# Adding the logarithm and relu terms of softplus on TensorE, by identity matmuls, instead of on VectorE

## Chip, cores and metric

The kernel runs on one core of a Trainium2 chip. The metric is the device time of one execution in microseconds (us), taken as the median of a few executions. A profile is one further execution, recorded by the hardware profiler.

## What is computed

The program is a network of two layers. Each layer has a state-space block (Mamba) over 2305 positions of 4 sequences, and then a mixture of experts. The change touches only the preparation of `dt` in the state-space block:

```python
dt = softplus(einsum('blr,dr->bld', dt, dt_proj_w) + dt_proj_b)     # the preparation
def step(h, (dt_t, B_t, C_t, u_t)):                                 # the scan over positions
    dA = exp(dt_t[:, :, None] * A)
    h = dA * h + (dt_t * u_t)[:, :, None] * B_t[:, None, :]
    y = einsum('bdn,bn->bd', h, C_t)
```

There are 128 inner channels and 16 states. softplus(v) is computed without overflow as relu(v) + ln(1 + e), with e = exp(-|v|). Because 1 + e is rounded, a correction rr = ((1 + e) - 1) - e is taken off the logarithm. So dt = ln(1 + e) - rr + relu(v).

## The kernel before

In each layer `phase_mamba` cuts every sequence into 5 chunks of 462 positions, so there are 20 chunks per layer and 40 in all. A chunk has 16 items (4 groups of channels by 4 groups of states, 128 rows each). The engines share an item like this, and each of them is a queue written out by hand, with semaphores between them:

- ScalarE writes the decay exp(dt*A) of the item into PSUM (line 647).
- GpSimd (POOL) forms the product dbu (line 700).
- VectorE scans decay and dbu over the positions (lines 782 and 785). For 10 items it multiplies the states by C itself, into `hc` (line 767). For the six items of `ON_POOL` GpSimd does it, into `hcp` (line 695).
- TensorE adds all 16 products into the PSUM bank `ysum` (line 558 for `hc`, 553 for `hcp`), in `SUM_ORDER`. The last three of that order are items 14 (`hc`), 13 (`hcp`) and 15 (`hc`).
- VectorE multiplies the finished `ysum` by the gate of the chunk (line 745), after the first scan of the next chunk.

While chunk k is scanned, chunk k+2 is prepared, spread over the queues by the `AT_` table. The preparation has a double PSUM buffer `front`: bank 0 takes the projections of u and dt, bank 1 those of z and of B and C. ScalarE writes `ab` = |v|, `rx` = relu(v) and `ex` = exp(-ab), then 1 + e into bank 0 (line 613), and after the decay of item 15 the logarithm into bank 1 (`prep_ln`, line 617). At the end of the chunk's program VectorE runs `prep_rr` (line 724) and `prep_dt` (line 731 takes `rr` off in PSUM, line 735 adds `rx` and writes `dd` in SBUF). GpSimd then multiplies `dd` by u (line 681), SyncE stores both to HBM and reads them back spread over the partitions as `rep`, and the next-but-one chunk scans with that. TensorE's next projection (`prep_u`, line 520) also waits for the end of `prep_dt`, since it overwrites `front`.

Two chunks are prepared before the loop (the prologue), in the same order of steps.

Of the kernel before, what the change touches and what calls it, by code (L numbers as in the profile page):

```python
# [14 lines left out]
ALU = mybir.AluOpType  # L15
ACT = mybir.ActivationFunctionType
AX_X = mybir.AxisListType.X

P = 128
# [13 lines left out]
TC = 462  # L33
# [21 lines left out]
HCD = 5  # L55


AT_SILU, AT_EXP, AT_ONE, AT_LN, AT_BC, AT_DT, AT_DTU, AT_Y = 6, 10, 11, 15, 13, 5, 3, 0
START = 16
NE, TOPK = 8, (2, 1)  # L60
F0, F1 = 512, 1024
# [14 lines left out]
def memory(nc, ctx, phase, used):  # L76

    def sb(name, shape, dt=F32):  # L80
        return ctx.enter_context(nc.sbuf_tensor(f"{phase}_{name}", shape, dt))

    def ps(name, shape, dt=F32):
        return ctx.enter_context(nc.psum_tensor(f"{phase}_{name}", shape, dt))

    def sem(name):
        used.append(nc.alloc_semaphore(f"{phase}_{name}"))
        return used[-1]

    return sb, ps, sem  # L90
# [297 lines left out]
def phase_mamba(nc, a, g, l):  # L388
# [4 lines left out]
    with ExitStack() as ctx:  # L393
        sb, ps, sem = memory(nc, ctx, f"mamba{l}", g["used"])
        T, m, sel = g["T"], g["mamba"][l], g["sel"]
        xs = sb("xs", [P, CW - 1])
        u, sz = sb("u", [P, UBUFS, TC]), sb("sz", [P, UBUFS, TC])
        ab, ex, rx, rr = sb("ab", [P, TC]), sb("ex", [P, TC]), sb("rx", [P, TC]), sb("rr", [P, TC])
        dd = sb("dd", [P, 2, TC])
        bc = sb("bc", [2 * DS, TC])  # L400

# [10 lines left out]
        ysum, front = ps("ysum", [P, BANK]), ps("front", [P, 2, BANK])  # L412

        xs_loaded, rep_loaded, bc_stored, dt_stored = sem("xs_loaded"), sem("rep_loaded"), sem("bc_stored"), sem("dt_stored")
        front_mm, front_act, front_dve, front_pool = sem("front_mm"), sem("front_act"), sem("front_dve"), sem("front_pool")
# [4 lines left out]
        y_ready, projected, added = sem("y_ready"), sem("projected"), sem("added")  # L420
        unshuffled, stats_ready, mv_ready = sem("unshuffled"), sem("stats_ready"), sem("mv_ready")
        half_ready, vare_ready, rstd_ready = sem("half_ready"), sem("vare_ready"), sem("rstd_ready")
        MM_U, MM_Z, MM_DT, MM_BC, MMS = 1, 2, 3, 4, 4
        A_U, A_Z, A_ABS, A_RELU, A_EXP, A_ONE, A_BC, A_LN, ACTS = 1, 2, 3, 4, 5, 6, 7, 8, 8
        D_R, D_LR, D_DT, DVES = 1, 2, 3, 3
        REPS = 2 * NS
        block = ctx.enter_context(nc.Block())

        def chunk_of(eng, tile, k):

            if isinstance(k, int):
                return tile[:, k % UBUFS, :]
            return tile[:, bass.ds(eng.snap(k % UBUFS), 1), :]
# [78 lines left out]
        @block.tensor  # L512
        def _(pe):
            for s in (front_mm, hc_summed, hcp_summed, projected):
                pe.sem_inc(s, START)

            def prep_u(k):
                pe.wait_ge(xs_loaded, 32 * (k + 1))
                pe.wait_ge(front_dve, START + DVES * k)
                nc.tensor.matmul(front[:, 0, 0:TC], m["wu"][:, 0, :], xs[:, 0:TC], start=True, stop=False)  # L520
                nc.tensor.matmul(front[:, 0, 0:TC], m["wu"][:, 1, :], xs[:, 2:2 + TC],
                                 start=False, stop=True).then_inc(front_mm, 1)

            def prep_z(k):
                nc.tensor.matmul(front[:, 1, 0:TC], m["wz"][:, :], xs[:, 2:2 + TC],
                                 start=True, stop=True).then_inc(front_mm, 1)

            def prep_dt(k):
                pe.wait_ge(front_act, START + ACTS * k + A_Z)
                nc.tensor.matmul(front[:, 0, 0:TC], m["wdt"][:, :], chunk_of(pe, u, k),  # L530
                                 start=True, stop=True).then_inc(front_mm, 1)

            def prep_bc(k):
                nc.tensor.matmul(front[0:2 * DS, 1, 0:TC], m["wbc"][:, :], chunk_of(pe, u, k),
                                 start=True, stop=True).then_inc(front_mm, 1)

            for k in range(2):
                prep_u(k)
                prep_z(k)
                prep_dt(k)  # L540
                prep_bc(k)
            with pe.Fori(0, NCH) as k:
                prep_u(k + 2)
                prep_z(k + 2)

                pe.wait_ge(y_ready, START + k)
                nc.tensor.matmul(ysum[:, 0:TC], m["diag"][:, :], chunk_of(pe, u, k), start=True, stop=False)
                for at, i in enumerate(SUM_ORDER):
                    end = at == ITEMS - 1
                    if i in ON_POOL:  # L550
                        n = ON_POOL.index(i)
                        pe.wait_ge(hcp_ready, START + NP_ * k + n + 1)
                        nc.tensor.matmul(ysum[:, 0:TC], sel[:, i // NM, :], hcp[:, n % HCP, :],  # L553
                                         start=False, stop=end).then_inc(hcp_summed, 1)
                    else:
                        n = ON_DVE.index(i)
                        pe.wait_ge(hc_ready, START + ND * k + n + 1)
                        nc.tensor.matmul(ysum[:, 0:TC], sel[:, i // NM, :], hc[:, n % HCD, :],  # L558
                                         start=False, stop=end).then_inc(hc_summed, 1)
                    if at == AT_DT:  # L560
                        prep_dt(k + 2)
                    if at == AT_DT + 1:
                        prep_bc(k + 2)

            pe.wait_ge(front_dve, START + DVES * (NCH + 2))
            for t in range(NT):
                b, j = divmod(t, TPB)
                pe.wait_ge(unshuffled, R * (b + 1))
                pe.wait_ge(added, START + t - 1)
                out = front[0:TT, t % 2, 0:C].rearrange("p (c q) -> p q c", q=R * R)  # L570
                for q in range(R * R):
                    mm = nc.tensor.matmul(out[:, q, :], yp[:, b % 2, q, j * TT:(j + 1) * TT], m["wout"][:, :],
                                          start=True, stop=True, skip_group_check=True)
                mm.then_inc(projected, 1)
# [8 lines left out]
        def _(act):  # L583
            act.sem_inc(front_act, START)
            act.sem_inc(decay_ready, START)
            at = act.alloc_register(f"act_row{l}")
# [26 lines left out]
                nc.scalar.activation(front[:, 0, 0:TC], ex[:, :], ACT.Copy, bias=1.0).then_inc(front_act, 1)  # L613

            def prep_ln(k):
                act.wait_ge(front_act, START + ACTS * k + A_BC)
                nc.scalar.activation(front[:, 1, 0:TC], ex[:, :], ACT.Ln, bias=1.0).then_inc(front_act, 1)

            def prep_bc(k):
                act.wait_ge(front_mm, START + MMS * k + MM_BC)  # L620
# [4 lines left out]
            for k in range(2):  # L625
                prep_silu(k)
                prep_exp(k)
                prep_one(k)
                prep_bc(k)
                prep_ln(k)  # L630
            nc.scalar.preload_act_table_set("exp_and_others")
            with act.Fori(0, NCH // 2) as pair:
                for par in range(2):
                    k = pair * 2 + par
# [82 lines left out]
        def _(dve):  # L717
# [8 lines left out]

            def prep_dt(k):
                done = START + DVES * k
                dve.wait_ge(front_act, START + ACTS * k + A_LN)
                dve.wait_ge(front_dve, done + D_R)  # L730
                nc.vector.tensor_tensor(front[:, 1, 0:TC], front[:, 1, 0:TC], rr[:, :], ALU.subtract).then_inc(front_dve, 1)
                if not (isinstance(k, int) and k == 0):
                    dve.wait_ge(dt_stored, 16 * NG * k)
                dve.wait_ge(front_dve, done + D_LR)
                nc.vector.tensor_tensor(dd[:, 0, :], front[:, 1, 0:TC], rx[:, :], ALU.add).then_inc(front_dve, 1)

            for k in range(2):
                prep_rr(k)
                prep_dt(k)
# [10 lines left out]
            with dve.Fori(0, B) as b:  # L750
# [4 lines left out]
                with dve.Fori(0, CPB) as c:  # L755
                    k = dve.snap(b * CPB + c)
# [17 lines left out]
                    for i in range(ITEMS):  # L774
                        done = START + ITEMS * k + i
# [15 lines left out]
                    read_out(ITEMS - 1)  # L791
                    prep_rr(k + 2)
                    prep_dt(k + 2)

            gate(NCH)
# [645 lines left out]
def build(nc, a):  # L1441
    with ExitStack() as ctx:
# [16 lines left out]
        for l in range(2):  # L1459
            phase_sequence(nc, a, g, l)  # L1460
            phase_mamba(nc, a, g, l)
            with ExitStack() as ffn:
                weights, phase_experts = ((weights0, phase_experts0), (weights1, phase_experts1))[l]
                g["xn"] = ffn.enter_context(nc.sbuf_tensor(f"xn{l}", [TT, NT, C], F32))
                w, prefetch = weights(nc, a, g, ffn)
                phase_route(nc, a, g, l, prefetch)
                phase_experts(nc, a, g, w)
            if l == 0:

                nc.clear_and_free_semaphores(g["used"])  # L1470
                g["used"].clear()
                nc.all_engine_barrier()  # L1472
# [40 lines left out]
```

## Time and profile before

| | |
|---|---|
| median of 3 executions | 2142.44 us (2141.5 to 2144.28) |
| the profiled execution's own time | 2142.27 us |
| its span in the profile | 2140.6 us |
| VectorE (DVE) busy | 1279.3 us, 60% |
| TensorE (PE) busy | 1574.8 us, 74% |
| GpSimd (POOL) busy | 1159.7 us, 54% |
| ScalarE (ACT) busy | 1027.7 us, 48% |

These are averages over a state-space loop and an experts stage in each layer, which have different limits. The page's 40 slices show VectorE at nine tenths or more through both state-space loops and at one or two tenths in much of the experts stages. "Idle before, releaser" in a row is how long the engine had nothing to do before the instruction, and what let it go on. A float32 matmul of the program is two records in the trace ("x2").

### The profile page before, as it was taken

How to read it: one execution, taken by the hardware profiler on the slowest of the kernel's cores; microseconds unless marked ns; L12 is line 12 of the kernel's file. 1: busy time of each engine (PE TensorE's matmuls, PEld its weight loads, DVE VectorE, ACT ScalarE, POOL GpSimd, SP SyncE). 2: the span in 40 equal slices, each digit the busy share in tenths (PEclk: the TensorE clock that was granted, in tenths of full speed). 3: DMA queues.
4: the chain of work that ended last, by engine and by line, in shares of the span. 5: the costliest groups of instructions: out<-in, count | busy, mean ns of one | idle time of the engine just before them, and what ended most of it. 6: DMA issues, size and time to landing. Idle time of an engine off the chain costs nothing. (4 is left out here: it accounts for less than half of the span.)

```text
span 2140.6 us, 26276 instructions
## 1 busy us (share of the span) xinstructions
PE 1574.8 (74%) x4872; PEld 813.1 (38%) x4873; DVE 1279.3 (60%) x2268; ACT 1027.7 (48%) x1696; POOL 1159.7 (54%) x1151
## 2 busy tenths in 40 slices
PE   4477777777786389999971367777777778199993
PEld 3122222222255146666640122222222228166661
DVE  4399999999976001111117279999999996111102
ACT  5577777777751022232321367777777762021111
POOL 2399999999941700000017179999999991400004
PEclk9799999999975699999995689999999995599995
DMA  6687777777735342111113487777777772123323
GB/s 215 145 177 175 174 176 175 174 174 173 170 85 194 92 137 69 44 44 47 47 47 99 122 181 175 173 177 176 173 174 174 171 170 88 55 71 112 111 65 97
DMA packets 104909, 283.48 MB, mean 132 GB/s; under 512 B 19788, under 2 KB 78428, under 8 KB 94012
## 3 DMA queue, kind: packets, MB, share of 16 engines
q1 hardware_dynamic: 96680, 265.34, 51.2%
q0 software_dynamic: 8192, 17.71, 2.8%
q8 instruction: 15, 0.25, 0.0%
q14 instruction: 22, 0.18, 0.0%
HBM read 225.80 MB, written 57.18 MB: 132 GB/s over the span
## 5 line engine op out<-in xcount | busy, mean ns | idle before, releaser
L700 POOL TENSOR_TENSOR mamba_dbu<-mamba_rep 128x462 f32<-128x462 f32 x640 | 676.4, 1084 | 69.7 <-DMA mamba_rep<-dt_rows 66.0
L558 PE MATMUL mamba_ysum<-mamba_hc,all_sel 128*128 128x462 f32 x800 | 420.6, 608 | 239.3 <-DVE mamba_hc L767 238.5
L647 ACT ACTIVATE mamba_state<-mamba_rep,all_m_acol 128x462 f32<-128x462 f32 x640 | 388.8, 638 | 228.1 <-DVE mamba_last L782 227.2
L785 DVE TENSOR_TENSOR_SCAN mamba_state<-mamba_state,mamba_carry,mamba_dbu 128x462 f32<-128x462 f32 x400 | 455.2, 1176 | 7.3 <-ACT mamba_state L647 7.3
L558 PEld LDWEIGHTS mamba_ysum<-mamba_hc,all_sel 128*128 128x128 f32 x800 | 125.9, 192 | 520.0 <-DVE mamba_hc L767 503.3
L782 DVE TENSOR_TENSOR_SCAN mamba_last<-mamba_state,mamba_last,mamba_dbu 128x462 f32<-128x462 f32 x240 | 280.7, 1170 | 30.2 <-ACT mamba_state L647 17.0
L695 POOL TENSOR_TENSOR mamba_hcp<-mamba_last,mamba_rep 128x462 f32<-128x462 f32 x240 | 266.6, 1111 | 35.0 <-DVE mamba_last L782 28.3
L1237 DVE TENSOR_TENSOR experts_h<-experts_sg,experts_up 128x512 f32<-128x512 f32 x62 | 42.6, 688 | 370.2 <-PE experts_up L1132 312.3
L767 DVE TENSOR_TENSOR mamba_hc<-mamba_state,mamba_rep 128x462 f32<-128x462 f32 x400 | 249.6, 627 | 0.0
L553 PE MATMUL mamba_ysum<-mamba_hcp,all_sel 128*128 128x462 f32 x480 | 238.3, 579 | 0.0
L290 POOL MEMSET seq_mhalf<- 96x3 f32 x2 | 0.2, 98 | 360.8 <-POOLq L1472 360.8
L1152 PE MATMUL experts_down<-weights_wd,experts_hT 128*128 x496 | 119.2, 384 | 40.1 <-issue 39.3
L553 PEld LDWEIGHTS mamba_ysum<-mamba_hcp,all_sel 128*128 128x128 f32 x480 | 90.9, 196 | 113.4 <-issue 110.5
L1152 PEld LDWEIGHTS experts_down<-weights_wd,experts_hT 128*128 128x128 f32 x496 | 95.1, 192 | 79.9 <-issue 69.9
L1384 POOL DMA_DIRECT2D expert_rows<-experts_eo x8 | 6.6, 826 | 217.2 <-DVE experts_eo L1374 217.2
L647 ACT ACT_TABLE_LOAD x80 | 102.6, 1283 | 38.2 <-DMA mamba_rep<-dt_rows 37.4
L1132 PE MATMUL experts_gate<-weights_wgu,experts_xT 128*128 x248 | 118.3, 600 | 3.5 <-ACT experts_xT L1188 2.9
L1207 ACT ACTIVATE experts_eo<-experts_down 128x256 f32<-128x256 f32 x62 | 23.8, 383 | 196.0 <-PE experts_down L1152 168.7
L1014 POOL DMA_INDIRECT slot_rows<-xn,all_slot x72 | 66.5, 923 | 94.0 <-issue 60.2
L1132 PE MATMUL experts_up<-weights_wgu,experts_xT 128*128 x248 | 116.7, 593 | 0.0
L1350 ACT ACTIVATE experts_hT<-experts_hid,weights_b 128x432 f32<-128x432 f32 x64 | 39.6, 620 | 156.0 <-PE experts_hid L1324 156.0
L1333 PE MATMUL experts_down<-weights_w,experts_hT 128*108 128x256 f32 x512 | 112.5, 380 | 1.2 <-ACT experts_hT L1350 0.7
(175 smaller groups left out, 2165.9 us busy)
## 6 DMA issues: line engine op xcount, KB each, us to landing
mamba_rep<-bc_rows SPq DMA_DIRECT2D x168, 462.0 KB, 7.0
mamba_rep<-dt_rows SPq DMA_DIRECT2D x168, 462.0 KB, 7.4
dt_rows<-mamba_dd SPq DMA_DIRECT2D x168, 115.5 KB, 7.6
weights_w<-in_L_w_dram SPq DMA_DIRECT2D x16, 1024.0 KB, 9.0
mamba_xs<-seq_scratch SPq DMA_DIRECT2D x92, 116.0 KB, 9.3
experts_xs<-slot_rows SPq DMA_DIRECT2D x62, 128.0 KB
expert_rows<-experts_eo SPq DMA_DIRECT2D x62, 128.0 KB, 1.7
slot_rows<-setup_zero SPq DMA_DIRECT2D x11, 512.0 KB
```

Of the source, the lines that this page charges most:

```text
L553: nc.tensor.matmul(ysum[:, 0:TC], sel[:, i // NM, :], hcp[:, n % HCP, :], start=False, stop=end).then_inc(hcp_summed, 1)
L558: nc.tensor.matmul(ysum[:, 0:TC], sel[:, i // NM, :], hc[:, n % HCD, :], start=False, stop=end).then_inc(hc_summed, 1)
L647: nc.scalar.activation(state[:, STATE_BANK[i], 0:TC], rep[:, par * REP_ROWS + i // NM, :], ACT.Exp, scale=m["acol"][:, i:i + 1]).then_inc( ...
L695: pool.tensor_tensor(hcp[:, n % HCP, :], last[:, n, :], rep[:, first + 3 * NG + i % NM, :], ALU.mult).then_inc(hcp_ready, 1)
L700: pool.tensor_tensor(dbu[:, i % 4, :], rep[:, first + NG + i // NM, :], rep[:, first + 2 * NG + i % NM, :], ALU.mult).then_inc(dbu_ready, 1)
L767: nc.vector.tensor_tensor(hc[:, n % HCD, :], state[:, STATE_BANK[i], 0:TC], rep[:, bass.ds(c_rows + 3 * NG + i % NM, 1), :], ALU.mult).the ...
L782: nc.vector.tensor_tensor_scan(last[:, n, :], bank, dbu[:, i % 4, :], last[:, n, TC - 1:TC], ALU.mult, ALU.add).then_inc(scan_done, 1)
L785: nc.vector.tensor_tensor_scan(bank, bank, dbu[:, i % 4, :], carry[:, i:i + 1], ALU.mult, ALU.add).then_inc(scan_done, 1)
L1014: pool.indirect_dma_start(out=g["xs"][:, :], out_offset=bass.IndirectOffsetOnAxis(ap=g["slot"][:, c, t:t + 1], axis=0), in_=g["xn"][:, t, ...
L1132: mm = nc.tensor.matmul(bank[:, par, :], xT[:, par, k * P:(k + 1) * P], wgu[:, bass.ds(e, 1), which, k, :], start=(k == 0), stop=(k == 1))
L1152: mm = nc.tensor.matmul(down[:, par, 0:C], hT[:, par, f * P:(f + 1) * P], wd[:, bass.ds(e, 1), f, :], start=(f == 0), stop=(f == FC0 - 1))
L1333: mm = nc.tensor.matmul(down[0:CT, i % 2, 0:C], hT[:, f, i * CT:(i + 1) * CT], w2[:, par, f, :], start=(f == 0), stop=(f == FC1 - 1))
```

## The change

TensorE gets a step `prep_add`: two matmuls with the identity as weights that put `ln` and `rx` into bank 1 of `front` and add them there. VectorE's pass of line 731 goes away, and its last pass takes `rr` off that sum. ScalarE writes the logarithm into a new SBUF tile `ln` instead of PSUM, and its wait in front of it goes away. `prep_add` stands on TensorE after the matmul at place 14 of `SUM_ORDER` (`AT_ADD`), which is item 13, and before that of item 15; it waits for the logarithm.

```diff
-AT_SILU, AT_EXP, AT_ONE, AT_LN, AT_BC, AT_DT, AT_DTU, AT_Y = 6, 10, 11, 15, 13, 5, 3, 0
+AT_SILU, AT_EXP, AT_ONE, AT_LN, AT_BC, AT_DT, AT_DTU, AT_Y, AT_ADD = 6, 10, 11, 15, 13, 5, 3, 0, 14
...
+            def prep_add(k):
+                pe.wait_ge(front_act, START + ACTS * k + A_LN)
+                nc.tensor.matmul(front[:, 1, 0:TC], g["ident"][:, :], ln[:, :], start=True, stop=False)
+                nc.tensor.matmul(front[:, 1, 0:TC], g["ident"][:, :], rx[:, :], start=False, stop=True).then_inc(front_mm, 1)
...
                 prep_bc(k)
+                prep_add(k)
...
                     if at == AT_DT + 1:
                         prep_bc(k + 2)
+                    if at == AT_ADD:
+                        prep_add(k + 2)
...
             def prep_ln(k):
-                act.wait_ge(front_act, START + ACTS * k + A_BC)
-                nc.scalar.activation(front[:, 1, 0:TC], ex[:, :], ACT.Ln, bias=1.0).then_inc(front_act, 1)
+                nc.scalar.activation(ln[:, :], ex[:, :], ACT.Ln, bias=1.0).then_inc(front_act, 1)
...
             def prep_dt(k):
                 done = START + DVES * k
-                dve.wait_ge(front_act, START + ACTS * k + A_LN)
-                dve.wait_ge(front_dve, done + D_R)
-                nc.vector.tensor_tensor(front[:, 1, 0:TC], front[:, 1, 0:TC], rr[:, :], ALU.subtract).then_inc(front_dve, 1)
+                dve.wait_ge(front_mm, START + MMS * k + MM_ADD)
                 if not (isinstance(k, int) and k == 0):
                     dve.wait_ge(dt_stored, 16 * NG * k)
-                dve.wait_ge(front_dve, done + D_LR)
-                nc.vector.tensor_tensor(dd[:, 0, :], front[:, 1, 0:TC], rx[:, :], ALU.add).then_inc(front_dve, 1)
+                dve.wait_ge(front_dve, done + D_R)
+                nc.vector.tensor_tensor(dd[:, 0, :], front[:, 1, 0:TC], rr[:, :], ALU.subtract).then_inc(front_dve, 1)
```

TensorE's queue at the end of the loop over chunks, before. The first row is item 14, then items 13 and 15.

```order
L558 MATMUL mamba_ysum<-mamba_hc,all_sel 128x462 [waits mamba0_hc_ready]
L552 REGISTER_ALU
L553 MATMUL mamba_ysum<-mamba_hcp,all_sel 128x462 [waits mamba0_hcp_ready]
L557 REGISTER_ALU
L558 MATMUL mamba_ysum<-mamba_hc,all_sel 128x462 [waits mamba0_hc_ready]
```

The same place in the changed kernel:

```order
L565 MATMUL mamba_ysum<-mamba_hc,all_sel 128x462 [waits mamba0_hc_ready]
L559 REGISTER_ALU
L560 MATMUL mamba_ysum<-mamba_hcp,all_sel 128x462 [waits mamba0_hcp_ready]
L539 REGISTER_ALU
L540 MATMUL mamba_front<-mamba_ln,all_ident 128x462 [waits mamba0_front_act]
L541 MATMUL mamba_front<-mamba_rx,all_ident 128x462
L564 REGISTER_ALU
L565 MATMUL mamba_ysum<-mamba_hc,all_sel 128x462 [waits mamba0_hc_ready]
```

The two adds stand behind the matmuls of items 14 and 13, and item 15 now stands behind the adds.

VectorE's queue at the end of the loop, before, from the product of item 15 on:

```order
L767 TENSOR_TENSOR mamba_hc<-mamba_state,mamba_rep 128x462 [waits mamba0_hc_summed]
L723 ISA
L724 SCALAR_TENSOR_TENSOR mamba_rr<-mamba_front,mamba_ex 128x462 [waits mamba0_front_act]
L729 REGISTER_ALU
L730 ISA [waits mamba0_front_act]
L731 TENSOR_TENSOR mamba_front<-mamba_front,mamba_rr 128x462 [waits mamba0_front_dve]
L733 REGISTER_ALU
L734 REGISTER_ALU [waits mamba0_dt_stored]
L735 TENSOR_TENSOR mamba_dd<-mamba_front,mamba_rx 128x462 [waits mamba0_front_dve]
L755 REGISTER_ALU
```

And in the changed kernel:

```order
L773 TENSOR_TENSOR mamba_hc<-mamba_state,mamba_rep 128x462 [waits mamba0_hc_summed]
L731 ISA
L732 SCALAR_TENSOR_TENSOR mamba_rr<-mamba_front,mamba_ex 128x462 [waits mamba0_front_act]
L737 ISA
L739 REGISTER_ALU [waits mamba0_front_mm]
L740 ISA [waits mamba0_dt_stored]
L741 TENSOR_TENSOR mamba_dd<-mamba_front,mamba_rr 128x462 [waits mamba0_front_dve]
L761 REGISTER_ALU
```

One pass is gone, and the one that is left waits for TensorE (`front_mm`); the loop's next scan stands behind it.

## Rows read from the trace of the kernel before

**Rows 1.** Windows: busy time per engine in the loops of both layers.

```profile
core 0: us, PE busy (x) PEld busy (x) DVE busy (x) ACT busy (x) POOL busy (x), PEclk, DMA share, GB/s
...
94.00:618.00 524.00, 403.28 (x879) 146.63 (x877) 511.73 (x727) 374.05 (x558) 484.95 (x459) 0.98 0.78 174
...
1245.00:1770.00 525.00, 404.09 (x878) 147.11 (x877) 511.68 (x727) 374.98 (x559) 484.16 (x459) 0.98 0.78 173
```

**Rows 2.** Groups by line: VectorE's two passes of `prep_dt`.

```profile
L731 DVE TENSOR_TENSOR mamba_front<-mamba_front,mamba_rr 128x462 f32<-128x462 f32 x44 | 28.5, 647 | 8.2 <-ACT mamba_front L617 6.8
...
L735 DVE TENSOR_TENSOR mamba_dd<-mamba_front,mamba_rx 128x462 f32<-128x462 f32 x44 | 28.1, 640 | 1.6
```

**Rows 3.** Timeline of VectorE over one chunk's end: start, us, instruction, [idle before].

```profile
277.27 1.18 DVE L782 TENSOR_TENSOR_SCAN mamba_last<-mamba_state,mamba_last,mamba_dbu 128x462 f32<-128x462 f32 x1 [0.32 <-issue]
...
300.54 0.64 DVE L767 TENSOR_TENSOR mamba_hc<-mamba_state,mamba_rep 128x462 f32<-128x462 f32 x1
301.09 0.64 DVE L724 SCALAR_TENSOR_TENSOR mamba_rr<-mamba_front,mamba_ex 128x462 f32<-128x462 f32 x1
301.76 0.65 DVE L731 TENSOR_TENSOR mamba_front<-mamba_front,mamba_rr 128x462 f32<-128x462 f32 x1
302.44 0.64 DVE L735 TENSOR_TENSOR mamba_dd<-mamba_front,mamba_rx 128x462 f32<-128x462 f32 x1
303.40 1.18 DVE L782 TENSOR_TENSOR_SCAN mamba_last<-mamba_state,mamba_last,mamba_dbu 128x462 f32<-128x462 f32 x1 [0.32 <-issue]
304.49 0.61 DVE L745 TENSOR_TENSOR mamba_y<-mamba_ysum,mamba_sz 128x462 f32 x1
```

**Rows 4.** Timeline of TensorE over the same end.

```profile
300.63 1.04 PE L558 MATMUL mamba_ysum<-mamba_hc,all_sel 128*128 128x462 f32 x2 [0.88 <-DVE mamba_hc L767]
301.51 0.94 PE L553 MATMUL mamba_ysum<-mamba_hcp,all_sel 128*128 128x462 f32 x2
302.28 0.94 PE L558 MATMUL mamba_ysum<-mamba_hc,all_sel 128*128 128x462 f32 x2
303.14 1.04 PE L520 MATMUL mamba_front<-mamba_xs,all_m_wu 128*128 128x462 f32 x2
```

**Rows 5.** Timeline of ScalarE there: the logarithm, then the next chunk's decays.

```profile
298.16 0.56 ACT L617 ACTIVATE mamba_front<-mamba_ex 128x462 f32<-128x462 f32 x1
...
300.47 1.78 ACT L647 ACTIVATE mamba_state<-mamba_rep,all_m_acol 128x462 f32<-128x462 f32 x3
```

**Rows 6.** Timeline of GpSimd there.

```profile
299.24 4.21 POOL L700 TENSOR_TENSOR mamba_dbu<-mamba_rep 128x462 f32<-128x462 f32 x4 [0.64 <-DMA mamba_rep<-dt_rows]
303.68 1.00 POOL L681 TENSOR_TENSOR mamba_dd<-mamba_dd,mamba_u 128x462 f32<-128x462 f32 x1 [0.23 <-issue]
```

**Rows 7.** Timeline: end of the first layer's loop, VectorE released by TensorE.

```profile
616.70 0.94 PE L558 MATMUL mamba_ysum<-mamba_hc,all_sel 128*128 128x462 f32 x2
...
617.67 0.64 DVE L745 TENSOR_TENSOR mamba_y<-mamba_ysum,mamba_sz 128x462 f32<-128x462 f32 x1 [0.17 <-PE mamba_ysum L558]
```

**Rows 8.** Timeline: the prologue of the first layer.

```profile
67.55 0.56 ACT L617 ACTIVATE mamba_front<-mamba_ex 128x462 f32<-128x462 f32 x1
...
68.82 0.64 DVE L735 TENSOR_TENSOR mamba_dd<-mamba_front,mamba_rx 128x462 f32<-128x462 f32 x1
...
69.60 1.88 PE L520 MATMUL mamba_front<-mamba_xs,all_m_wu 128*128 128x462 f32 x2 [6.65 <-DVE mamba_dd L735]
...
71.28 1.75 PE L521 MATMUL mamba_front<-mamba_xs,all_m_wu 128*128 128x462 f32 x2
...
83.73 0.65 DVE L731 TENSOR_TENSOR mamba_front<-mamba_front,mamba_rr 128x462 f32<-128x462 f32 x1 [1.70 <-ACT mamba_front L617]
...
84.48 0.64 DVE L735 TENSOR_TENSOR mamba_dd<-mamba_front,mamba_rx 128x462 f32<-128x462 f32 x1
```

**Rows 9.** Windows and timeline of TensorE: a low-clock stretch (columns: busy, clock, DMA share, GB/s).

```profile
284.61:285.61 1.00, 1.00 (x3) 0.50 0.47 91
...
284.54 1.75 PE L553 MATMUL mamba_ysum<-mamba_hcp,all_sel 128*128 128x462 f32 x2
```

More of the change, by code:

```diff
@@ L398, in phase_mamba @@
         ab, ex, rx, rr = sb("ab", [P, TC]), sb("ex", [P, TC]), sb("rx", [P, TC]), sb("rr", [P, TC])
+        ln = sb("ln", [P, TC])
         dd = sb("dd", [P, 2, TC])
@@ L422, in phase_mamba @@
         half_ready, vare_ready, rstd_ready = sem("half_ready"), sem("vare_ready"), sem("rstd_ready")
-        MM_U, MM_Z, MM_DT, MM_BC, MMS = 1, 2, 3, 4, 4
+        MM_U, MM_Z, MM_DT, MM_BC, MM_ADD, MMS = 1, 2, 3, 4, 5, 5
         A_U, A_Z, A_ABS, A_RELU, A_EXP, A_ONE, A_BC, A_LN, ACTS = 1, 2, 3, 4, 5, 6, 7, 8, 8
-        D_R, D_LR, D_DT, DVES = 1, 2, 3, 3
+        D_R, D_DT, DVES = 1, 2, 2
         REPS = 2 * NS
```

## The prediction

> **What bounds the kernel now.** I first read the page's slices: VectorE is full only in the two state-space loops, and the change touches nothing else. The windows of these loops [rows 1] give the limit there: VectorE is busy 511.73 of 524 us and 511.68 of 525 us, next to 485 us of GpSimd, 403 us of TensorE and 374 us of ScalarE. So an added or removed microsecond on VectorE, busy or waiting, is a microsecond of the kernel, as long as no other engine takes over. The timeline of VectorE over one chunk [rows 3] shows the period: the first scan of one chunk starts at 277.27 us and that of the next at 303.40 us, so 26.13 us a chunk. The reader should look at its last four instructions: the product of item 15 (300.54), `rr` (301.09 to 301.73), the pass of line 731 (301.76) and that of line 735 (302.44 to 303.08). The next scan starts at 303.40, which is 0.96 us after line 735 started. There is hardly an idle gap. Then I read the other queues at the same moment, since the new pass waits for one of them: TensorE [rows 4], ScalarE [rows 5], GpSimd [rows 6].
>
> **The change, part by part.**
>
> *VectorE loses line 731.* It lasts 0.647 us [rows 2] and its successor starts 0.68 us after it (301.76 to 302.44, [rows 3]). Taken alone this gives 40 x 0.68 = 27 us back. The pass that is left reads PSUM and SBUF and writes SBUF, as line 735 does now, so it takes 0.64 us [rows 2].
>
> *ScalarE.* The logarithm goes to SBUF instead of PSUM, 0.56 us [rows 5]. It ends at 298.72 and nothing asks for it before 301.7, so the other destination and the dropped wait cost nothing. The cover is 3 us; the decays that follow have their own cover, since those of the next chunk start at 300.47 for a scan at 303.40.
>
> *TensorE gets two matmuls, and where they stand decides the case.* Their inputs are there early, but the queue is in order: they stand behind the matmul of item 14, which waits for VectorE's product of that item and starts at 300.63 [rows 4], and behind that of item 13 (301.51). Item 15 starts at 302.28, and there the first add will start. Price of an add: it is a float32 matmul of 128x128 weights by 462 columns, the shape of lines 553 and 558, and one that follows another starts 302.28 - 301.51 = 0.77 us after it; the last one's end is 0.94 us after its start [rows 4]. So the `ln` add starts at 302.28, the `rx` add at 303.05 and ends at 303.99. That the weights are the identity changes nothing in it that a row shows, so the 0.77 us of the row goes into the sum. The Trainium skill (TensorE: Matmul & The Clock Gate, Back-to-back issue gap) gives N/2.4 + 2.5 ns for a matmul at full clock, which for N = 462 is an estimated 0.195 us; by that the adds would end about 1.2 us earlier and the loop's part of the sum would be some 20 us. The trace does not agree for float32: its 0.77 us is four times as much. The skill's FP8 and Floating Point Precision (TensorE Precision Notes) gives true FP32 four passes, and with those the trace agrees.
>
> *The new wait on VectorE.* How soon VectorE goes on after TensorE is in the rows at the loop's end [rows 7]: the last matmul ends at 616.70 + 0.94 = 617.64 and the gate starts at 617.67, 0.03 us later. In the changed queue a wait and a further wait instruction stand between the semaphore and the pass. The nearest row is in the prologue [rows 8]: line 731 ends at 84.38 and line 735, with such an instruction ahead of it, starts at 84.48, 0.10 us later, against 0.03 us in the loop. I take 0.10, with 0 and 0.2 as bounds. So the pass starts at 303.99 + 0.10 = 304.09. Line 735 starts at 302.44 now. Everything behind it (the 0.96 us to the next scan, the loop's branch and registers) moves with it, so the chunk gets 304.09 - 302.44 = **1.65 us longer** (1.55 to 1.75), the missing pass already counted: VectorE ends `rr` at 301.73 and then waits 2.36 us for something that replaces 0.68 us. This recurs in every one of the 40 chunks: 40 x 1.65 = **66.0 us** (62 to 70).
>
> *What queues behind, and who is late next.* Behind the waiting pass on VectorE are all scans of the next chunk. TensorE's item 15 moves to 303.83 to 304.77; its reader is the gate, now at 304.49 [rows 3], which moves with the scans to 306.14, so 1.3 us are left. TensorE's next projection (303.14, [rows 4]) waits for the pass, so it moves by the same 1.65 us, to 304.79, and item 15 is just done. GpSimd's product of `dd` starts at 303.68 now [rows 6] and cannot start before about 304.8, so +1.1 us, and its stores and the `rep` transfer behind it move by as much. The transfer lands 0.64 us after GpSimd asks for it (299.24), and the decays it feeds begin at 300.47 [rows 5], for a scan at 303.40. The first is over at about 301.1 (1.78/3 = 0.6), so 2.3 us are spare; it arrives 1.1 later, and the scan that needs it comes 1.65 later, so the margin grows. No second stall follows. All other work in a chunk hangs on VectorE's scans and moves with them.
>
> *The prologue.* For chunk 0 the chain is logarithm, `prep_dt`, GpSimd, store, replicate, first scan, and VectorE waits at its end anyway. The logarithm ends at 68.11 and line 735 starts at 68.82 [rows 8]. Afterwards the adds start at about 68.18. TensorE will have been idle for over 5 us, and after 6.65 us of idleness the row at 69.60 is at the low clock: 1.68 us to the next pair's start, and that pair 1.75 us. At those rates the adds end at 68.18 + 3.43 = 71.61 and the pass starts at 71.71, so +2.9 us; at the full clock of [rows 4] (0.88 + 0.94) it is +1.3. I take the low clock, 2 layers x 2.9 = **5.8 us** (2.6 to 5.8). Chunk 1's preparation moves too, but ends before the replicated rows of chunk 0 arrive.
>
> *The sum.* 66.0 + 5.8 = 71.8 us. Against the profiled execution's own time, 2142.27 us, this is 2214.1 us; the median of the runs shown is 0.2 us above that, so 2214.2, and I say 2214.
>
> **The rivals.**
>
> 1. *Forecast, slower by about 72 us.* Chance 0.84. Its own range is 62 + 2.6 to 70 + 5.8, so 2207 to 2218; a few chunks with a low clock at their end (rival 2's price of 3.1 us, three times) make the upper end 2227.
>
> 2. *TensorE's clock falls at the end of the chunk.* Now a chunk in the loop has a low stretch in some places early in it: clock 0.50, which is 1.2 GHz, and a pair of 1.75 us in place of 0.94 [rows 9], behind a stretch in which TensorE mostly waited for VectorE's products. It costs nothing there, because no one waits for these sums. If that met the four matmuls that the pass now waits for, they would take 1.68 + 1.54 + 1.54 + 1.75 = 6.5 us in place of 3.36, +3.1 us each time. The windows have the mean clock at 0.98 in the loops [rows 1], so about 4% of 1049 us, 42 us, is at the low level. A low microsecond on these matmuls delays VectorE by half a microsecond, so if all of it fell there the kernel would lose 21 us more, 2235 us; in every chunk it would be 124 us. Against it: the chunk's end is TensorE's densest part, and the period changes only by 6%. Chance 0.06.
>
> 3. *The other side: the adds are hidden.* If they ended before `rr` does (301.73), the missing pass would be pure gain: 2142.4 - 27 = 2115 us, less 1 for the prologue. For that they would have to end 2.3 us earlier than I find; a saving starts where they end before about 302.3 (the pass would start before 302.44). That needs them ahead of item 14's wait in the queue, since even item 14's and item 13's matmuls take until 302.28. The order of the changed program has them behind. It stays possible only if the modelled ends and starts of the matmuls mislead by over 1.6 us. Chance 0.04.
>
> 4. *An add is cheaper than the row*: one record and not two, half the price, 0.39 us each. The pass then starts 0.77 us earlier, 0.88 us per chunk, 35 us and some 4 us in the prologue, 2181 us. All matmuls of this shape are two records [rows 4], so 0.04. (The skill's formula above would make an add cheaper still, and the estimate some 2165 us.)
>
> 5. *It cancels out.* VectorE's delay would have to be taken from a wait elsewhere in the loop; its idle time in the whole loop is 12 us of 524 [rows 1]. 2142 us, chance 0.02.
>
> **How the numbers follow.** The likeliest case gives 2214. The range 2205 to 2227 holds it with its bounds and a few low-clock ends, and leaves out rivals 2 to 5 (0.16). A change within 0.2% (4 us) is what a measurement of this kernel can hardly tell from none. Slower: rivals 1, 2 and 4, 0.94. Within 0.2%: 0.02. Faster: 0.04.
>
> **What the profile of the changed kernel would show.** The period between first scans near 27.8 us; the last VectorE pass of a chunk with about 2.3 us idle before it, released by TensorE; that wait about 94 us over 40 chunks; the adds starting 1.65 us after item 14's start with 0.77 us between them; GpSimd's product of `dd` waiting for VectorE; VectorE's busy time down by 44 x 0.647 = 28.5 us, while the span grows. I would be wrong if the adds showed a start before 302.28 relative to item 14, or if a wait for the `rep` transfer appeared on VectorE's first scan.

## The result, and the profile after

The changed kernel takes 2215.07 us (median of 4 runs, 2212.71 to 2216.69), the kernel before 2141.97 us (median of 4, 2138.43 to 2144.28). The ratio is 1.0342, with a 95% interval of 1.0324 to 1.036: the change makes the kernel 73 us slower. The prediction said 2214 us, slower.

The first thing to look at is the end of a chunk on VectorE in the changed kernel. This timeline answers to [rows 3]; its columns are start, us, instruction, [idle before].

```profile
289.94 1.18 DVE L788 TENSOR_TENSOR_SCAN mamba_last<-mamba_state,mamba_last,mamba_dbu 128x462 f32<-128x462 f32 x1 [0.33 <-issue]
...
313.21 0.64 DVE L773 TENSOR_TENSOR mamba_hc<-mamba_state,mamba_rep 128x462 f32<-128x462 f32 x1
313.76 0.64 DVE L732 SCALAR_TENSOR_TENSOR mamba_rr<-mamba_front,mamba_ex 128x462 f32<-128x462 f32 x1
316.90 0.64 DVE L741 TENSOR_TENSOR mamba_dd<-mamba_front,mamba_rr 128x462 f32<-128x462 f32 x1 [2.50 <-PE mamba_front L541]
317.87 1.18 DVE L788 TENSOR_TENSOR_SCAN mamba_last<-mamba_state,mamba_last,mamba_dbu 128x462 f32<-128x462 f32 x1 [0.33 <-issue]
318.96 0.61 DVE L751 TENSOR_TENSOR mamba_y<-mamba_ysum,mamba_sz 128x462 f32 x1
```

Where `rr` was followed at once by two passes, it is followed by 2.50 us of nothing and one pass. From the product of item 15 to the last pass it is now 316.90 - 313.21 = 3.69 us; it was 1.90. The period, from first scan to first scan, is 317.87 - 289.94 = 27.93 us in place of 26.13, so 1.80 us more. It is the same in all chunks but those in which a new sequence starts (0.4 us longer, before and after alike) or the loop has just begun (up to 0.2 us longer).

TensorE at the same place answers to [rows 4]:

```profile
313.30 1.04 PE L565 MATMUL mamba_ysum<-mamba_hc,all_sel 128*128 128x462 f32 x2 [0.88 <-DVE mamba_hc L773]
314.18 0.94 PE L560 MATMUL mamba_ysum<-mamba_hcp,all_sel 128*128 128x462 f32 x2
314.95 0.94 PE L540 MATMUL mamba_front<-mamba_ln,all_ident 128*128 128x462 f32 x2
315.73 0.94 PE L541 MATMUL mamba_front<-mamba_rx,all_ident 128*128 128x462 f32 x2
316.50 0.94 PE L565 MATMUL mamba_ysum<-mamba_hc,all_sel 128*128 128x462 f32 x2
317.59 1.04 PE L521 MATMUL mamba_front<-mamba_xs,all_m_wu 128*128 128x462 f32 x2 [0.15 <-DVE mamba_dd L741]
```

The adds stand where the order of the queue put them: items 14 and 13 first, then the two adds at distances of 0.77 us, and item 15 behind. The inputs of the adds had been ready since the logarithm's end, at 310.83 + 0.59 = 311.42 in the timeline of ScalarE:

```profile
310.83 0.59 ACT L625 ACTIVATE mamba_ln<-mamba_ex 128x462 f32<-128x462 f32 x1
```

The groups by line, with the idle time ahead of them and its releaser, give the sum over all chunks:

```profile
L689 POOL TENSOR_TENSOR mamba_dd<-mamba_dd,mamba_u 128x462 f32<-128x462 f32 x42 | 45.7, 1088 | 157.5 <-DVE mamba_dd L741 157.5
...
L540 PE MATMUL mamba_front<-mamba_ln,all_ident 128*128 128x462 f32 x88 | 45.2, 597 | 20.9 <-ACT mamba_ln L625 20.9
L541 PE MATMUL mamba_front<-mamba_rx,all_ident 128*128 128x462 f32 x88 | 44.5, 590 | 0.0
L741 DVE TENSOR_TENSOR mamba_dd<-mamba_front,mamba_rr 128x462 f32<-128x462 f32 x44 | 28.2, 640 | 120.9 <-PE mamba_front L541 120.9
```

VectorE waited 120.9 us for the second add: four times 5.23 us in the prologues, and 100 us in the 40 chunks. TensorE waited for the logarithm only in the prologues, 4 times 5.2 us. VectorE's busy time fell from 1279.3 to 1251.1 us, as it had to, and the kernel got slower.

Where the 74.4 us between the two profiled spans (2215.0 and 2140.6 us) are, by the timelines of VectorE: from the first scan to the last gate of a loop it was 523.99 and 523.77 us and is 559.66 and 559.53 us, so 71.4 us are in the two loops. The two stretches from the first `rr` to the first scan are 0.2 and 0.8 us shorter (27.88 to 27.66 us, and 28.39 to 27.59), which is about as much as traces with the same prologue differ: e5 below, whose prologue is that of the kernel before, has 27.23 and 27.66 us. The remaining 4.0 us are spread over stages that the change does not touch; the four executions after lie 4 us apart themselves.

### The profile page after: what moved, and what is told of

The parts are those of the page before. It is cut to its first block and busy times, and to the rows that moved or that the text cites. A ratio compares the mean times of both kernels' runs of the same rounds, so it can differ in the third digit from the quotient of the medians.

```text
span 2215.0 us, 26542 instructions
## 1 busy us (share of the span) xinstructions
PE 1656.1 (75%) x5048; PEld 852.1 (38%) x5049; DVE 1251.1 (56%) x2224; ACT 1029.1 (46%) x1696; POOL 1159.6 (52%) x1151
## 5 line engine op out<-in xcount | busy, mean ns | idle before, releaser
L689 POOL TENSOR_TENSOR mamba_dd<-mamba_dd,mamba_u 128x462 f32<-128x462 f32 x42 | 45.7, 1088 | 157.5 <-DVE mamba_dd L741 157.5
L1356 ACT ACTIVATE experts_hT<-experts_hid,weights_b 128x432 f32<-128x432 f32 x64 | 39.7, 620 | 156.5 <-PE experts_hid L1330 156.5
```

## The experiments

Ten kernels were run. Each is compared with the kernel before on the same chip, because the chips differ: the kernel before took 2093.68 and 2095.46 us on two of them and 2139.81 us on a third. The time saved on the faster chips is in the stretches outside the two loops: e7 below, run on one of them, has the changed kernel's period of 27.93 us, and its loops take 559.59 and 559.50 us, where the changed kernel's took 559.66 and 559.53. So the table gives the difference of the medians on one chip, and the period between first scans that most chunks of the trace have. e7 is not in it, since it was executed once only.

| kernel | median, us | before, same chip | difference | ratio (95%) | period |
|---|---|---|---|---|---|
| changed kernel | 2215.07 | 2141.97 | +73.1 | 1.0342 (1.0324 to 1.036) | 27.93 |
| e3 adds behind item 15 | 2195.83 | 2093.68 | +102.2 | 1.0491 (1.0472 to 1.0509) | 28.70 |
| e2 adds ahead of item 13 | 2136.58 | 2093.68 | +42.9 | 1.0205 (1.0188 to 1.0222) | 27.15 |
| e1 adds ahead of item 14 | 2076.4 | 2093.68 | -17.3 | 0.9912 (0.9898 to 0.9927) | 25.67 |
| e4 TensorE's wait last | 2156.78 | 2093.68 | +63.1 | 1.0303 (1.0284 to 1.0322) | 27.72 |
| e5 wait, no adds | 2167.77 | 2139.81 | +28.0 | 1.0122 (1.0106 to 1.0139) | 26.84 |
| e6 one add | 2179.49 | 2139.81 | +39.7 | 1.0187 (1.017 to 1.0204) | 27.15 |
| e9 pass removed, nothing added | 2118.18 | 2139.81 | -21.6 | 0.9898 (0.9881 to 0.9914) | 25.56 |
| e10 e1, wait last, gate later | 2119.03 | 2139.81 | -20.8 | 0.9904 (0.9887 to 0.992) | 25.57 |
| e11 e1, gate later | 2069.13 | 2095.46 | -26.3 | 0.9875 (0.9858 to 0.9891) | 25.46 |

The main theory (A) was that the place of the adds in TensorE's queue is the cost. Its rival (B) was that handing work to TensorE, or its added work, costs wherever it stands.

**e1, e2, e3: the place alone.** One number of the table that sets the order is changed.

```diff
-..., AT_Y, AT_ADD = 6, 10, 11, 15, 13, 5, 3, 0, 14
+..., AT_Y, AT_ADD = 6, 10, 11, 15, 13, 5, 3, 0, 12      # e1; 13 in e2, 15 in e3
```

e1, ahead of item 14:

> Theory A (the place in TensorE's queue): the adds now stand ahead of item 14's matmul, so they start when item 11's is done, 299.58 us in the terms of the trace of before, and end at 301.29, before rr ends at 301.73. VectorE's last pass follows rr with no wait, the chunk loses the missing pass, 0.68 us: period 25.45 us, and 40 x 0.68 = 27 us less than the kernel before, 2115 us. Theory B (TensorE's part costs as such: the handover to it, or its added 1.7 us of work per chunk): the pass still waits about as in the changed kernel, period 27.9, 2215 us. Theory C (the place matters, but something else becomes the bound once VectorE is shorter: GpSimd, busy 24 us of a period, or the replicated rows): between 2120 and 2142 us with a new wait on VectorE's scans.

e2, between items 14 and 13:

> The adds stand between item 14's matmul and item 13's, one matmul earlier than in the changed kernel. Theory A: VectorE's pass starts 0.77 us earlier in each chunk, period 27.93 - 0.77 = 27.16 us, 40 x 0.77 = 31 us less than the changed kernel, 2184 us. Theory B: no difference, 2215 us.

e3, behind item 15:

> The adds stand behind item 15's matmul, one matmul later than in the changed kernel. Theory A: period 27.93 + 0.77 = 28.70 us, 31 us more than the changed kernel, 2246 us. Theory B: no difference, 2215 us.

Measured: the periods of e2 and e3 are 27.15 and 28.70 us, 0.78 less and 0.77 more than the changed kernel, one matmul each way. e1 is faster than the kernel before. So the same two matmuls, the same handover and the same VectorE work give +102, +73, +43 or -17 us by their place alone, and B falls. But e1 has 25.67 us in most chunks and 25.45 only in a few, 17 us gained and not 27: C is partly true, though neither of its candidates is. The wait is not on a scan: the first scan still starts 0.96 us behind the last pass, as before, and the 0.32 us of idle time in its row, which the profile puts down to ScalarE here, was there before too [rows 3]. VectorE's and TensorE's timelines in e1 show where the rest went. The adds end at 271.19 + 0.94 = 272.13, before `rr` does (272.56), and the pass follows `rr` at once, as expected:

```profile
271.93 0.63 DVE L732 SCALAR_TENSOR_TENSOR mamba_rr<-mamba_front,mamba_ex 128x462 f32<-128x462 f32 x1
272.59 0.64 DVE L741 TENSOR_TENSOR mamba_dd<-mamba_front,mamba_rr 128x462 f32<-128x462 f32 x1
273.55 1.18 DVE L788 TENSOR_TENSOR_SCAN mamba_last<-mamba_state,mamba_last,mamba_dbu 128x462 f32<-128x462 f32 x1 [0.32 <-ACT mamba_state L655]
274.85 0.64 DVE L751 TENSOR_TENSOR mamba_y<-mamba_ysum,mamba_sz 128x462 f32 x1
...
271.19 0.94 PE L541 MATMUL mamba_front<-mamba_rx,all_ident 128*128 128x462 f32 x2
...
273.52 0.94 PE L565 MATMUL mamba_ysum<-mamba_hc,all_sel 128*128 128x462 f32 x2
```

The gate (line 751) starts 1.30 us after the first scan; before it was 1.09 [rows 3]. It needs the sum with item 15, whose matmul ends at 273.52 + 0.94 = 274.46, just before the gate would have been due (274.64), with three instructions of VectorE's queue between that wait and the gate. Nothing marks it as idle in the row; the reader finds it by comparing starts. That this delay is what is missing is tested by e10 and e11.

**e4: the order of VectorE's waits.** In the changed kernel the pass starts 316.90 - (315.73 + 0.94) = 0.23 us after the second add's modelled end, where I had taken 0.10.

```diff
-                dve.wait_ge(front_mm, START + MMS * k + MM_ADD)
                 if not (isinstance(k, int) and k == 0):
                     dve.wait_ge(dt_stored, 16 * NG * k)
                 dve.wait_ge(front_dve, done + D_R)
+                dve.wait_ge(front_mm, START + MMS * k + MM_ADD)
```

> The changed kernel with the three waits of VectorE's last pass in another order: the wait for TensorE is the last and sits on the pass itself, so no wait instruction stands between the semaphore and the pass. In the changed kernel the pass starts 0.23 us after the second add's modelled end. If the two instructions in between are part of that, it starts 0.03 to 0.1 us after it, period 27.73 to 27.80, 5 to 8 us less than the changed kernel, 2207 to 2210 us. If the 0.23 us is the handover itself, the period stays 27.93 and the time 2215 us.

```profile
287.21 0.64 DVE L741 TENSOR_TENSOR mamba_dd<-mamba_front,mamba_rr 128x462 f32<-128x462 f32 x1 [2.30 <-PE mamba_front L541]
...
286.23 0.94 PE L541 MATMUL mamba_front<-mamba_rx,all_ident 128*128 128x462 f32 x2
```

Now it is 287.21 - 287.17 = 0.04 us, the period is 27.72 us, 0.21 less, and the difference to the kernel before is 63 us in place of 73. Two instructions of the queue are gone from between TensorE's semaphore and the pass, the one that carried this wait (line 739) and the one with the wait for the stores (line 740); together they cost 0.2 us, so 0.1 us each. The handover itself costs next to nothing. The 10 us are more than the 5 to 8 expected; the two differences come from different chips, and 40 times the 0.21 us is 8.

The order in the code is not always that of the queue. In the prologues, where the waits are for constants and not for registers, it is the other way round: the pass starts 0.04 us after the second add in the changed kernel and 0.11 to 0.14 us after it in e4, whose trace has a wait instruction between them there.

**e5: the wait without the adds.** The kernel before, with one more wait in front of line 731.

```diff
                 dve.wait_ge(front_dve, done + D_R)
+                if not isinstance(k, int):
+                    dve.wait_ge(hcp_summed, START + NP_ * (k - 1))
                 nc.vector.tensor_tensor(front[:, 1, 0:TC], front[:, 1, 0:TC], rr[:, :], ALU.subtract).then_inc(front_dve, 1)
```

> The kernel before, both VectorE passes kept, no adds on TensorE; only the first pass (line 731) also waits until TensorE has summed item 13. Theory A (order of TensorE's queue): that matmul ends at 302.45 us in the trace of before, and with no instruction between the wait and the pass VectorE starts 0.03 us later, 302.48, where it starts at 301.76: 0.72 us per chunk, period 26.85, 29 us more than the kernel before. With the 0.23 us seen in the changed kernel it would be 0.9 us and 37 us. Theory B (the adds themselves, through TensorE's load, clock or PSUM): no adds, so no difference to the kernel before.

Measured: period 26.84 us, 0.71 us more than before, +28 us. Theory A's figure was 0.72 and 29 us. The first pass (here line 733) starts 0.03 us after item 13's matmul ends (278.70 + 0.94 = 279.64):

```profile
278.29 0.63 DVE L724 SCALAR_TENSOR_TENSOR mamba_rr<-mamba_front,mamba_ex 128x462 f32<-128x462 f32 x1
279.67 0.65 DVE L733 TENSOR_TENSOR mamba_front<-mamba_front,mamba_rr 128x462 f32<-128x462 f32 x1 [0.75 <-PE mamba_ysum L553]
...
278.70 0.94 PE L553 MATMUL mamba_ysum<-mamba_hcp,all_sel 128*128 128x462 f32 x2
```

Without any work added to TensorE, being behind item 13 alone costs VectorE this much.

**e6: one add.** The changed kernel without the second matmul (the relu term is left out of dt).

> The changed kernel with one identity matmul instead of two: the relu term is left out of dt. If an add costs a whole float32 matmul of 0.77 us on the way to VectorE, the period falls from 27.93 to 27.16 us and the time is 43 us above the kernel before, in place of 73. If the handover and the wait for item 13 are the cost and the adds are nearly free, it stays within 5 us of the changed kernel.

Measured: period 27.15 us, 0.78 less than in the changed kernel, +39.7 us (43 expected; 40 times the 1.02 us over the period before is 41). The price of an add on this path is a whole float32 matmul. So the changed kernel's loop adds up from measured parts: e5's wait behind item 13 (0.71), two adds (2 x 0.78), two instructions behind the wait (0.21), less the missing pass (0.68), 1.80 us, which is what the periods say.

**e9: the pass removed and nothing in its place.** The kernel before without line 731 (the correction `rr` is left out of dt; it is still computed).

> The kernel before without VectorE's pass of line 731 and with nothing in its place (the correction rr is left out of dt). This is the most that taking one pass off VectorE can bring: theory A expects 0.68 us per chunk, period 25.45, 27 us below the kernel before. If another engine or the replicated rows bound the shorter chunk, the period is above 25.45 and VectorE's first scan waits for them.

Measured: 25.56 us and -21.6 us, not 25.45 and -27. Neither an engine nor the replicated rows are late, since the first scan starts 0.97 us behind the last pass, as ever. The last pass starts 0.75 us after `rr`, in place of 0.66 in e1:

```profile
271.04 0.62 DVE L724 SCALAR_TENSOR_TENSOR mamba_rr<-mamba_front,mamba_ex 128x462 f32<-128x462 f32 x1
271.79 0.64 DVE L733 TENSOR_TENSOR mamba_dd<-mamba_front,mamba_rx 128x462 f32<-128x462 f32 x1
272.76 1.18 DVE L780 TENSOR_TENSOR_SCAN mamba_last<-mamba_state,mamba_last,mamba_dbu 128x462 f32<-128x462 f32 x1 [0.33 <-ACT mamba_state L647]
```

In my edit the wait for the stores stood behind the wait for `rr`. It is the 0.1 us of e4 again, now behind another wait; no run of this kernel with the waits exchanged was made, but e10 and e11 differ in that way alone.

**e10 and e11: the gate one scan later.** Both have e1's place and `AT_Y` = 1; e10 also has e4's order of waits, e11 that of the changed kernel.

```diff
-..., AT_Y, AT_ADD = 6, 10, 11, 15, 13, 5, 3, 0, 14
+..., AT_Y, AT_ADD = 6, 10, 11, 15, 13, 5, 3, 1, 12
```

> The changed kernel with the adds ahead of item 14, the wait for TensorE last, and the gate one scan later in VectorE's queue. With the adds ahead of item 14 the period was mostly 25.67 us and not 25.45, and the gate started 1.30 us after the chunk's first scan in place of 1.09, since TensorE ended item 15 only just before. If that late sum is all that was missing, the gate behind the second scan finds it done, the period is 25.45 in nearly all chunks, and the time is 26 to 28 us below the kernel before, against 17 us with the gate where it was. If GpSimd or the replicated rows hold the chunk, it stays at 25.67 and 17 us.

Measured for e10: 25.57 us in nearly every chunk, -20.8 us, between the two outcomes that were expected. The gate's delay is gone, but the last pass starts 0.77 us after `rr`: with the adds early, `rr` and not TensorE comes last, and e4's order puts an instruction behind that wait. So e11:

> The changed kernel with the adds ahead of item 14 and the gate one scan later, and VectorE's three waits in the order of the changed kernel, so that the wait for rr sits on the pass itself. With the wait for TensorE last the pass started 0.76 us after rr, with this order and the adds ahead 0.66 us. If each instruction between the wait that ends last and the pass costs 0.1 us, the period falls from 25.57 to about 25.46 us and the time is 24 to 26 us below the kernel before, against 21 us. If the other rows' order does not matter, it stays at 25.57 and 21 us.

```profile
270.85 0.62 DVE L732 SCALAR_TENSOR_TENSOR mamba_rr<-mamba_front,mamba_ex 128x462 f32<-128x462 f32 x1
271.51 0.64 DVE L741 TENSOR_TENSOR mamba_dd<-mamba_front,mamba_rr 128x462 f32<-128x462 f32 x1
272.46 1.18 DVE L788 TENSOR_TENSOR_SCAN mamba_last<-mamba_state,mamba_last,mamba_dbu 128x462 f32<-128x462 f32 x1 [0.31 <-ACT mamba_state L655]
273.56 1.16 DVE L791 TENSOR_TENSOR_SCAN mamba_state<-mamba_state,mamba_carry,mamba_dbu 128x462 f32<-128x462 f32 x1
274.63 0.62 DVE L751 TENSOR_TENSOR mamba_y<-mamba_ysum,mamba_sz 128x462 f32 x1
```

Measured: 25.46 us, -26.3 us, ratio 0.9875. The last pass follows `rr` by 0.66 us and the gate is not late. This is the gain that taking one pass off VectorE can bring (0.68 us x 40 = 27 us), and e11 beats both kernels.

**e7: a longer prologue.** In the changed kernel the prologue got no longer, against my 5.8 us. The queue of SyncE shows why; its rows are the issues of transfers. Before:

```profile
67.91 1.73 SPq L468 DMA_DIRECT2D mamba_rep<-bc_rows  x4
70.72 2.59 SPq L461 DMA_DIRECT2D dt_rows<-mamba_dd  x4
80.33 1.72 SPq L476 DMA_DIRECT2D mamba_rep<-dt_rows  x4
```

After:

```profile
68.22 1.73 SPq L469 DMA_DIRECT2D mamba_rep<-bc_rows  x4
73.89 2.60 SPq L462 DMA_DIRECT2D dt_rows<-mamba_dd  x4
80.51 1.72 SPq L477 DMA_DIRECT2D mamba_rep<-dt_rows  x4
```

Counted from the first `rr` (65.80 us before, 66.12 after), the stores of dt are issued 2.9 us later (7.77 us in place of 4.92), but the replication that waits for them is issued 0.1 us earlier (14.39 in place of 14.53). In e7 TensorE does two extra `ln` matmuls in front of the adds, in the prologue alone; nothing else changes.

```diff
                 prep_bc(k)
+                pe.wait_ge(front_act, START + ACTS * k + A_LN)
+                for _ in range(2):
+                    nc.tensor.matmul(front[:, 1, 0:TC], g["ident"][:, :], ln[:, :], start=True, stop=True)
                 prep_add(k)
```

> The changed kernel with two more identity matmuls ahead of the adds of the two chunks of the prologue, nothing else; about 3.1 us more on that chain at the low clock. In the changed kernel the chain got 3.2 us longer at the stores of dt, but the first scan still came 27.7 us after the first rr, as before (27.9). Theory D (the dt rows' stores wait behind the transfer that replicates B and C, so the first 3 us are hidden, and only what goes beyond shows): the first scan comes 29 to 31 us after the first rr. Theory E (nothing of this chain is on the path to the first scan): it stays at 27.4 to 28.2 us. The loop's period is 27.93 us in either.

```profile
68.39 1.73 SPq L469 DMA_DIRECT2D mamba_rep<-bc_rows  x4
76.61 2.60 SPq L462 DMA_DIRECT2D dt_rows<-mamba_dd  x4
80.94 1.72 SPq L477 DMA_DIRECT2D mamba_rep<-dt_rows  x4
```

e7 was executed once (2168.97 us), so only its trace is used. Its stores are issued 10.32 us after the first `rr` (66.29 us), 5.4 us later than before and 2.5 us later than in the changed kernel, and the replication of dt at 14.65 us after it. From the first issue of these stores to that of the replication the three kernels took 9.6, 6.6 and 4.3 us in the first layer and 9.9, 6.3 and 5.6 us in the second. From the issue of the B and C replication to that of dt they took 12.4, 12.3 and 12.6 us in the first layer, and 12.7, 12.0 and 13.5 us in the second. So all of the changed kernel's 2.9 us was hidden in front of the replication in both layers. Of e7's further delay of the stores 0.3 of 2.5 us reached the replication in the first layer, and 1.5 of 2.2 us in the second. In the first layer the stores themselves took a median of 8.0, 5.1 and 2.6 us from issue to landing, and from 70 to 76 us the profile has the DMA engines fully busy in all three traces, at 219 to 232 GB/s. That fits theory D, that the stores wait behind that transfer; whether by their order in the queue or because the engines are busy is open, since neither the queues nor the transfer were changed.

The first scan comes 28.5 and 29.3 us after the first `rr` in the two layers. The first is short of D's range of 29 to 31, and both are above E's 28.2. In the changed kernel it was 27.7 and 27.6 us, and the other traces lie between 27.2 and 28.0 us in the first layer and between 27.5 and 28.4 in the second. The period stayed at 27.93 us.

## Why the prediction was right, step by step

**What bounds the kernel.** Right: in every variant of the table the time moved by about 40 times what VectorE's period moved by, within 2.1 us.

**The place of the adds and their price.** Right. The wait for item 14's product, item 13's matmul and 0.77 us per add appear as worked out, and e2, e3 and e6 measure single matmuls on this path (0.78, 0.77 and 0.78 us) and e5 the wait behind item 13 without the adds (0.71 us). The quick formula of the Trainium skill (TensorE: Matmul & The Clock Gate, Back-to-back issue gap), by which an add would have been an estimated 0.2 us, does not give the float32 matmuls here, which measure 0.77 to 0.78.

**The new wait's latency.** This term was mis-sized: 0.10 us taken, 0.23 measured, and above the bound of 0.2. The row that I used had one instruction behind the wait, the changed loop has two, line 739 with the wait itself and line 740 (e4). With it the period grew by 1.80 and not 1.65 us, and the loops by 71.4 and not 66.0 us; 1.80 also lies just above my 1.55 to 1.75.

**The prologue.** Wrong in its effect: the chain up to the stores did get 2.9 us longer, as worked out, at the low clock (the adds took 68.51 to 71.95, 3.44 us against my 3.43), but the step "VectorE waits at its end anyway", taken to mean that the delay reaches the first scan, failed. The replication behind the stores was issued no later; the stores seem to wait for another transfer, which fits e7 but is not proven. 5.8 us predicted, none found (0.2 and 0.8 us less).

These two errors have opposite signs. The loops came out 5.4 us over, the prologues 6.8 us under, and the stages outside, for which I had said nothing, gave 4.0 us more in the profiled pair. That the total of 2214 is within 1 us of the median is in part luck; the direction and the size of the loop's term are not.

**What queues behind.** Right: item 15 and the gate moved with the scans (the gate 1.09 us after the first scan, as before), TensorE's projection 0.15 us behind item 15's end, and no new wait for replicated rows held VectorE: four first scans of a sequence have 0.56 us of idle time put down to a replication, but 0.56 us stands before such scans in the kernel before too, with other releasers. GpSimd waited for `dd` 40 times (4 times before), which cost nothing, as the first scan still follows the last pass by 0.97 us.

**The rivals.** A clock drop at the chunk's end did not occur: every chunk has the same 3.14 us from `rr` to the pass. The rival on the other side, adds ahead of item 14's wait, is what e1 builds, and it gives 17.3 us and not the 27 that I gave it (2115 us). There the missing pass was not pure gain, because item 15's sum, now behind the adds, came late for the gate by 0.2 us a chunk, which I had not worked out for this rival. With the gate one scan later (e11) it is 26.3 us.

## What to carry to other kernels

Moving work from the bounding engine to an idle one helps only if the result is back before the bounding engine asks for it. The idle engine's queue is in order, so read what stands ahead of the new work there: here two matmuls that wait for the bounding engine's own late products made a saving of 27 us a loss of 73. Then look at the new engine's other readers, and put the wait that is fulfilled last on the instruction itself, behind the waits that are fulfilled early.

## What the runs showed that I had not expected

- On VectorE each instruction of the queue from the wait that is fulfilled last up to the pass, if that wait is not on the pass itself, costs 0.1 us: 0.23 us from the add's end to the pass with two of them, 0.04 with none (e4); 0.77 us from `rr` to the pass with one, 0.66 with none (e10, e11). Over 40 chunks that is 4 us for one instruction's place in the queue.
- Line 735's successor, the next scan, starts 0.95 to 0.98 us behind the last pass's start in all kernels, whatever came ahead of it, but for the first chunks of a loop (1.0 us, once 1.53 in e11) and of a sequence (1.36).
- A chain in the prologue that is 5.4 us longer at its stores delayed the first scan by only 0.6 and 0.9 us in the two layers (28.5 after 27.9, 29.3 after 28.4), where traces with the same prologue differ by up to 0.7 us.
